# Prologue of an attention-and-experts layer: statistics, input sums and weight sums of the Strassen projection moved between engines, and the first group written anew

## The reference

```python
xn = layernorm(x)                                  # x: 2 x 2048 x 2048, over the last axis, fp32
q, k, v = split(xn @ Wqkv + bqkv)                  # 2048 -> 3 x 512
attn = softmax(q @ k.T / sqrt(512)) @ v
att = attn @ Wo + bo                               # 512 -> 2048
scores = (xn @ Wq.T) @ keys.T                      # 64 experts, router width 16
gate = softmax over the 16 largest of 64 scores, 0 elsewhere
z = (xn @ A.T).reshape(64, 8) * gate               # 64 experts of rank 8
out = x + att + 2 * z.reshape(512) @ B.T
```

## Time and profile before

| | |
|---|---|
| median of 3 runs | 2947.73 us (2945.4 to 2949.84) |
| time of the profiled execution | 2944.45 us |
| its span, first to last instruction | 2942.6 us |
| busy: PE / DVE / ACT / POOL | 94% / 63% / 32% / 25% of the span |
| chain of work that ended last | PE 74%, DVE 11%, DMA 5%, issue 4%, ACT 2%, POOL 2% |
| data moved | 476.34 MB, 162 GB/s on average; first fortieth of the span 373 GB/s |

### The profile page before, as it was taken

The page is one execution under the profiler, slowest core; times in us unless marked ns, Lnnn a source line. Parts: engine busy times, 40 slices in busy tenths (PEclk is TensorE's granted clock), DMA queues, the critical chain, the costliest instruction groups (busy, mean ns, idle before and its releaser), DMA issues.

```text
span 2942.6 us, 34127 instructions
## 1 busy us (share of the span) xinstructions
PE 2774.7 (94%) x12096; PEld 2252.9 (77%) x12096; DVE 1860.2 (63%) x2133; ACT 931.4 (32%) x1164; POOL 733.5 (25%) x429
## 2 busy tenths in 40 slices
PE   2888999999999999999979999999999999999999
PEld 1666787878778787888868787787887878878787
DVE  5776777676776777364565665656656565565653
ACT  1222232323232223322343343333433434334331
POOL 7165213020120303020030503305033050330511
PEclk8989999999999999999989999999999999999999
DMA  9667455544554554324524534545344353444544
GB/s 373 233 232 241 153 190 166 187 137 152 191 180 143 165 172 143 115 96 148 180 77 129 192 110 149 165 128 185 109 151 167 128 178 116 144 170 129 175 138 137
DMA packets 261611, 476.34 MB, mean 162 GB/s; under 512 B 26864, under 2 KB 76016, under 8 KB 257264
## 3 DMA queue, kind: packets, MB, share of 16 engines
q1 hardware_dynamic: 223408, 372.45, 38.8%
q10 hardware_dynamic: 29376, 68.72, 6.7%
q0 software_dynamic: 8704, 33.56, 3.2%
HBM read 390.74 MB, written 83.91 MB: 161 GB/s over the span
## 4 chain that ended last, share of the span: by engine, by line
PE 74%; DVE 11%; DMA 5%; issue 4%; ACT 2%; POOL 2%; SPq 2%; DVEq 0%; ACTq 0%; POOLq 0%
PE psum L694 30%; PE psum L1478 14%; PE psum L1480 13%; PE psum L1479 13%; DVE prob L1675 2%; DVE w_lo L744 2%; PE psum L631 2%; DVE r_lo L1647 2%; ACT r_hi L1359 1%; DMA t_scratch<-xb 1%; DVE s_lo L749 1%; SPq L363 1%; DVE part L731 1%; DMA w_raw<-t_scratch 1%; DVE xb L765 1%
## 5 line engine op out<-in xcount | busy, mean ns | idle before, releaser
L744 DVE TENSOR_TENSOR w_lo<-w_raw,w_hi 128x1024 fp32r<-128x1024 f32 x224 | 321.4, 1435 | 408.3 <-ACT w_hi L445 408.0
L445 ACT ACTIVATE w_hi<-w_raw 128x1024 fp32r<-128x1024 f32 x224 | 237.4, 1060 | 937.6 <-PE psum L694 807.1
L1647 DVE TENSOR_TENSOR r_lo<-r_raw,r_hi 128x1024 fp32r<-128x1024 f32 x256 | 383.1, 1510 | 190.4 <-ACT r_hi L1359 190.4
L1478 PE MATMUL psum<-r_hi,f_hi 128*128 128x512 f32 x1024 | 406.8, 397 | 27.6 <-DVE r_lo L1647 26.2
L1480 PE MATMUL psum<-r_hi,f_lo 128*128 128x512 f32 x1024 | 402.1, 393 | 0.0
L1479 PE MATMUL psum<-r_lo,f_hi 128*128 128x512 f32 x1024 | 402.1, 393 | 0.0
L694 PE MATMUL psum<-s_hi,w_hi 128*128 128x512 f32 x896 | 355.7, 397 | 43.4 <-DVE w_lo L744 30.2
L1613 POOL TENSOR_TENSOR res<-res,b_out 128x512 f32<-128x512 f32 x128 | 218.5, 1736 | 664.6 <-DMA res<-x 664.4
L694 PE MATMUL psum<-w_hi,s_hi 128*128 128x512 f32 x896 | 353.9, 395 | 27.8 <-DVE w_lo L744 27.8
L694 PE MATMUL psum<-w_lo,s_hi 128*128 128x512 f32 x896 | 352.3, 393 | 0.0
L694 PE MATMUL psum<-w_hi,s_lo 128*128 128x512 f32 x896 | 352.1, 393 | 0.0
(11 more groups left out here) (133 smaller groups left out, 4290.9 us busy)
## 6 DMA issues: line engine op xcount, KB each, us to landing
w_raw<-t_scratch SPq DMA_DIRECT2D x128, 512.0 KB, 3.9
w_raw<-W_blocks SPq DMA_DIRECT2D x96, 512.0 KB, 3.9
r_raw<-k_scratch SPq DMA_DIRECT2D x64, 512.0 KB, 3.8
r_raw<-v_scratch SPq DMA_DIRECT2D x64, 512.0 KB, 5.5
r_raw<-B_T SPq DMA_DIRECT2D x64, 512.0 KB, 3.9
res<-x SPq DMA_DIRECT2D x128, 256.0 KB, 4.9
r_raw<-Wo SPq DMA_DIRECT2D x64, 512.0 KB, 4.4
out<-res SPq DMA_DIRECT2D x128, 256.0 KB, 3.4
```

Source lines behind the costliest of these rows:

```text
L445: nc.scalar.activation(w_hi[:, s % RAW], w_raw[:, s % RAW], ACT.Copy).then_inc(s_whi, 1)
L744: nc.vector.tensor_tensor(w_lo[:, s % RAW], w_raw[:, s % RAW], w_hi[:, s % RAW].bitcast(F32), ALU.subtract).then_inc(s_wlo, 1)
L1478: pe.matmul(bank, sh, mh, start=first, stop=False)
L1647: nc.vector.tensor_tensor(r_lo[:, slot, :], r_raw[:, slot, :], r_hi[:, slot, :].bitcast(F32), ALU.subtract).then_inc(b_lo, 1)
```

## The change

- **Constants and first loads.** The host lays `WqT` out as 128 rows of 256 numbers, in the order in which the partitions hold them; SP issues the constants first, then weight 0 and weight 1 after the second and the fourth tile of `x` have landed. ACT loads block 0 of x behind the four tiles, and splits the router's weight before the first square root. DVE finishes the router's weight after its first tile.
- **Statistics.** For the tiles of groups 1 to 3, and for tiles 4, 6 and 7 of the first group, the sums are made by ACT (`moments`: Identity with a sum, mean, negated mean, Square with a sum, variance) instead of DVE; ACT no longer waits for DVE before a rows load. `STATS_AT` is spaced otherwise, and in the first group store and broadcast stand two items later.
- **Input sums.** s3, s4, s2 and s1 are made by DVE, in every group: in pass 1 (s3, s4), pass 4 (s2), pass 5 (s1); in the first group, pass 1, in the order of `MIX0`.
- **Weight sums.** In the first group DVE makes them from the `w_raw` that is there for the product anyway and one or two quarters that POOL has loaded: t3 beside pass 2, t4 and t2 beside pass 3, t1 beside pass 5. SP stores them. SP's reload of a `w_raw` slot waits for the sum as well.
- **GpSimd** issues transfers only: blocks 2 and 3 of x, then the 32 loads of weight quarters.

```diff
+SUMMED = {2: ("t3",), 3: ("t2", "t4"), 5: ("t1",)}
-STATS_AT = [(1, 1), (1, 2), (1, 3), (1, 4), (2, 1), (2, 2), (2, 3), (3, 1)]
+STATS_AT = [(1, 1), (1, 2), (1, 5), (2, 1), (2, 2), (2, 3), (2, 5), (2, 6)]
+MIX0 = [((2, 0),), ((3, 0), "s3"), ("s4", (2, 1)), ((3, 1), "s3"), ("s4", (2, 2)), ((3, 2), "s3"), ("s4", (2, 3)),
+        ((3, 3), "s3"), ("s4",)]
+OWN_AT = {(0, 3): 4, (0, 5): 6, (0, 6): 7}
...
         def load_w(g, idx, s):
             n = item(g, idx, s)
             wait(sp, s_wlo, n - RAW + 1)
+            if static(g) and g == 0:
+                i, k = (idx, s - RAW) if s >= RAW else (idx - 1, s - RAW + IPI)
+                if i in SUMMED:
+                    sp.wait_ge(s_tsum, t_number(i, k))
...
         def constants():
-            sp.dma_start(wq_raw[:], WqT.rearrange("(k p) r -> p k r", p=P)).then_inc(s_const, 16)
+            sp.dma_start(wq_raw[:].rearrange("p k r -> p (k r)"), WqT).then_inc(s_const, 16)
...
+        constants()
+        sp.wait_ge(s_row0[1], 16)
         load_w(0, 0, 0)
-        for p in range(PART):
-            sp.dma_start(x_pair(0, p), xT[2 * p * P:(2 * p + 2) * P, 0:W].rearrange("(a p) t -> p a t", p=P)
-                         ).then_inc(s_x[0][p], 16)
+        sp.wait_ge(s_row0[HT - 1], 16)
         load_w(0, 0, 1)
-        constants()
...
+        def moments(g, j):
...
+            chain = Chain(act, s_moments, base)
+            act.wait_ge(s_rows[j % 2], 16 * loads)
+            chain.link(nc.scalar.activation(tile, tile, ACT.Identity, accum_out=total[:, col]))
+            chain.step(nc.scalar.activation(mv[:, 0, col], total[:, col], ACT.Copy, scale=1.0 / C))
+            chain.link(nc.scalar.activation(less_mean[:, col], total[:, col], ACT.Copy, scale=-1.0 / C))
+            chain.link(nc.scalar.activation(tile, tile, ACT.Square, bias=less_mean[:, col], accum_out=squares[:, col]))
+            chain.link(nc.scalar.activation(var[:, col], squares[:, col], ACT.Copy, scale=1.0 / C))
+            act.sem_inc(s_amv, 1)
...
+        def sum_weights(idx, s):
+            dve.wait_ge(s_tload[s % PART], 16 * (t_uses(idx, s) + 1))
+            if idx == 3:
+                dve.wait_ge(s_tload1[s % PART], 16 * (s // PART + 2))
+                nc.vector.tensor_tensor(row_tile(s), w_raw[:, s % RAW], row_tile(s), ALU.add).then_inc(s_tsum, 1)
+                dve.wait_ge(s_tsum, t_number(3, s) - 1)
+                nc.vector.tensor_tensor(t_tile(3, s), t_tile(3, s), row_tile(s), ALU.subtract).then_inc(s_tsum, 1)
+            elif idx == 2:
+                nc.vector.tensor_tensor(t_tile(2, s), w_raw[:, s % RAW], t_tile(2, s), ALU.subtract).then_inc(s_tsum, 1)
...
+                        if s == 6:
+                            dve.wait_ge(s_mv, HT + 1)
+                            rstd_ready(len(OWN_AT), slice(HT, NTOK))
+                        if s == 7:
+                            rstd_finish(2, (HT + 1) * TILE_STEPS + RSTD_STEPS, slice(HT, NTOK))
...
+                    if not first and idx == 1 and 1 <= s <= PART:
+                        s3(g, s - 1)
+                        s4(g, s - 1)
+                    if idx == 4 and 1 <= s <= PART:
+                        s2(g, s - 1)
+                    if idx == 5 and 1 <= s <= PART:
+                        s1(g, s - 1)
...
+        def load_b21_b11(s):
+            stored(2, PART + s) if s < PART else stored(3, s - PART)
+            load_summand(3, s, "b21")
+            if s == 0:
+                pool.wait_ge(s_amv, len(OWN_AT) + NTOK)
...
+            pool.dma_start(row_tile(s), w_block("b11", s // PART, s % PART)).then_inc(s_tload1[s % PART], 16)
...
-        "WqT": np.ascontiguousarray(np.transpose(L0_ffn_Wq_w)),
+        "WqT": np.ascontiguousarray(np.transpose(L0_ffn_Wq_w).reshape(C // P, P, -1).transpose(1, 0, 2)).reshape(P, -1),
```

More of the change, by code:

```diff
@@ L164, in phase_a @@
     GATE_STEPS = 4 * HT + 6
-    T_ITEMS = 2 * HK
+    STAT_STEPS = 5
     def sb(name, shape, dt=F32):
@@ L490, in x_load, with rows_load @@
                           .rearrange("(a p) t -> p a t", p=P)).then_inc(s_x[block][p], 16)
-        def rows_load(g, j, tiles):
-            wait(act, s_tiles, tiles)
+        def rows_load(g, j):
             act.dma_start(rows[:, j % 2, :], x[bass.ds(g * TG + j * P, P), :]).then_inc(s_rows[j % 2], 16)
+        def moments(g, j):
+            tile = rows[:, j % 2, :]
+            col = slice(j, j + 1)
+            if static(g) and g == 0:
+                base, loads = max(j - HT - 1, 0) * STAT_STEPS, (j - HT) // 2 + 1
+            else:
+                base, loads = (g * NTOK - NTOK + len(OWN_AT) + j) * STAT_STEPS, g * HT - HT // 2 + j // 2 + 1
+            chain = Chain(act, s_moments, base)
[6 more added lines that the diff above has]
+            act.sem_inc(s_amv, 1)
         def square_roots(event, cols):
@@ L515, in scalar @@
             act.dma_start(first_rows(j), x[j * P:(j + 1) * P, :]).then_inc(s_row0[j], 16)
+        for p in range(PART):
+            x_load(0, 0, p)
+        act.wait_ge(s_const, 64)
+        act.wait_ge(s_wq, 1)
+        nc.scalar.activation(wq[:, :, 0:RD], wq_raw[:], ACT.Copy).then_inc(s_wq, 1)
         square_roots(1, slice(0, HT))
@@ L521, in scalar @@
                 split_weights(0, 0, 0)
-        rows_load(0, HT, 1)
-        rows_load(0, HT + 1, 0)
-        for p in range(PART):
-            x_load(0, 1, p)
         split_x(0, 0, 0)
@@ L550, in body @@
                         split_x(g + 1, 0, s - PART - 1)
+                    if first and (idx, s) in OWN_AT:
+                        moments(0, OWN_AT[idx, s])
                     if idx == 0 and s == PART - 1:
@@ L908, in norm_count @@
                 return NORM0.index((block, p)) + 1
+            if static(g) and g == 1:
+                return 4 * PART + NORM1.index((block, p)) + 1
             return g * 4 * PART + NORM.index((block, p)) + 1
@@ L935, in body @@
                         split_weights(g + 1, 0, 0)
+                    if first and (idx, s) == (2, 0):
+                        s4(0, PART - 1)
+                    if first and s + 1 < IPI and idx in SUMMED:
+                        sum_weights(idx, s + 1)
+                    if first and s + 1 == IPI and idx + 1 in SUMMED:
+                        sum_weights(idx + 1, 0)
                     if s == 0:
@@ L1100, in stored @@
+        for s in range(IPI):
+            load_b12(s)
+        for s in range(IPI):
+            load_b21_b11(s)
+        for s in range(IPI):
+            load_b22(s)
     def stored(engine):
```

311 lines of the change are left out of this document (156 added, 155 removed).

## The result

The changed kernel takes **2878.21 us**, median of 4 runs (2874.43 to 2878.93), against 2946.57 us before (4 runs, 2944.66 to 2949.84): a ratio of 0.9764, 95% interval 0.9747 to 0.9781. The forecast was 2868 us, with a range of 2840 to 2903. Its profiled execution took 2878.93 us, span 2877.1.

A forecast was written before the change was run, and what follows sets the result against it. PE was busy 94% of the span, so time could come only from stretches with PE idle or slow. The terms -9.5 - 25 - 10 - 10 - 5 - 17 = -76.5 us, against 2944.45, gave 2868 us; range 2840 to 2903.

The forecast's parts named there:

- The start: Up to the first product: earlier tiles and faster DVE additions bring it from 41.5 to 32 us, -9.5 us.
- pass 0: First group's pass 0: the 20.4 us wait for the router's weight goes; 78.0 to 53 us, -25 us.
- Pass 1: First group: 12.2 us new idle time behind store and broadcast, yet 72.8 to 63 us, -10 us.
- "1 us" for DVE's work behind the wait: Pass 1, after the broadcast: DVE's 4.8 to 7.2 us per item beside PE's 5.4 to 6.3 cost about 1 us.
- the rival with DVE as the bound: Passes 1 and 3: 16 items each take 1.5 us more, late loads +6; 2898 us; chance 0.14.
- Pass 3: First group: a late load costs 4 us, DVE's sums and gating 1.5; 57.2 to 52 us, -5 us.
- one late load: Pass 3's first sum needs a load POOL issues only after ACT's last moments; 4 us charged.
- Groups 1 to 3: Later groups: no DVE addition held up by POOL, 8 of 22.4 us of waits left, no slow spells; -17 us.
- ACT's cover: Groups 1 to 3: ACT's added 38 us of moments stay hidden behind 3.1 us of slack.
- The constants: Rival at the start: constants wait for bandwidth, not their rows; first product at 86 instead of 32; 2922 us; chance 0.06.
- POOL's issues: Costed at nothing; rival in pass 3: DVE holds them up, 3.3 us each; 2878 us; chance 0.03.
- the slower rival: Moments too long, in 27 places between weight copies; decides from about 10.3 us; at 11 us 2963 us; chance 0.02.

The follow-up runs named there:

- rows_behind: Changed kernel; first group's two 1 MB rows loads for the next group issued behind pass 1's statistics broadcast instead of between store and broadcast: 2870.56 us (0.9743).
- no_store_wait: Changed kernel; first group's second half of tokens normalised with the first half's statistics, broadcast three items later: 2871.14 us (0.9734).
- half_loads: Changed kernel; in pass 3 of the first group GpSimd loads only the first 128 of each 256 rows of b21 and b11: 2866.96 us (0.9726).
- half_sums: Changed kernel; in pass 3 of the first group an item's two sums cover 512 instead of 1024 columns: 2874.68 us (0.9752).
- sums_on_pool: Changed kernel; input sums s3, s4, s2, s1 of groups 1 to 3 back on GpSimd in the old order: 2913.14 us (0.9882).

## Why the prediction was right, and where it was not

**The start (-9.5, measured -10.6) and pass 0 (-25, measured -26.4).** Confirmed with their steps: the last statistics end at 20 us, the first additions take 1.22 us, ACT had the constants at 9.55 us. The wait for the router's weight went, and nothing as large came next.

**Pass 1 (-10, measured -3.7).** The new idle time was foreseen at its place: 13.3 us against 12.2. By the profile the store took 8.8 us instead of 11.5 and the broadcast 9.7 instead of 5.0: two errors that nearly cancel. The term fell short behind that: PE was idle 18.1 us instead of 14, since it also waited 4.1 us at the end of the pass for the router's result, and busy 51.0 instead of 49. The step that failed is "1 us" for DVE's work behind the wait. What came of it is mainly that wait of 4.1 us: DVE reads the router's result behind its normalising and its sums, and the first product of pass 2 waits for this. From the broadcast to the end of the pass DVE has hardly a gap, 44.16 of 47.22 us:

```profile
104.38:151.60 47.22, 39.51 (x160) 31.24 (x161) 44.16 (x39) 21.56 (x28) 2.17 (x3) 0.90 0.62 204
```

So here the rival with DVE as the bound had the mechanism, though not the 12 us that it charged for the pass. With DVE as the bound behind the wait, a us less of the wait is worth at least a us of the pass: rows_behind took 4.0 off the wait and 5.6 off the pass, no_store_wait 6.7 and 7.8.

**Pass 2 (-10, measured -9.5).** Confirmed.

**Pass 3 (-5, measured +11.8). This is the step that failed.** It counted DVE's instructions and one late load, "landing, at most the 6.8 us that twice the bytes take", and never the transfers of the pass as a whole. That could have been done from the rows: 0.5 MB of weight, 1 MB of quarters and 1 MB of sums an item are 20 MB (21.0 million bytes), and at the 378 GB/s of the start 55 us, longer than the 52 forecast, before results and chains are added. At the 330 GB/s that the pass reached it is 64 us, and all that moved in its 69.0 us is 22.8 million bytes. half_loads shows that the transfers are the bound; half_sums excludes DVE. The late load for which 4 us were charged cost DVE 1.97. The second part is the broadcast: it had 5 us in the sum for pass 1 and nothing for pass 3, where its store now takes 22.6 us instead of 11.1, in front of ACT's weights.

**Groups 1 to 3 (-17, measured -30).** The mechanism was right, the size too small. Of the 22.4 us of waits for low weights 4.0 are left, not 8, and waits of 3.5 us for a part (L924) went besides: 21.9 us. PE's busy time for the same matmuls, the slow spells after the waits, fell from 976.5 to 970.1 us in the three groups, 6.4 us, where the -17 left 2.6 for it beside 14.4 of waits. Together these are 28 of the 30 us. ACT's cover held: 133.55 of 325.4 us busy.

**The rest.** The 2 us more of passes 4 to 6 hold a wait of 1.53 us for a low weight just ahead of group 1.

**The rivals.** DVE as the bound was right for pass 1 in kind, and refuted for pass 3, which did become longer, but by its transfers. The constants came early. POOL's issues took 0.72 us in pass 3, with DVE making two additions an item: not held up, as the sum had it. The Trainium skill ("SBUF — State Buffer", section SBUF: two separate sides) states that GpSimd can't write its transfers' descriptors while DVE runs an instruction in a 2-port performance mode, and that an instruction with two inputs in SBUF competes only with a GpSimd instruction that reads SBUF. These additions have two inputs in SBUF, so for them it states no hold-up of the issues, and the trace agrees (0.72 us); that additions on both engines do hold each other up agrees as well (DVE's 2.62 us beside POOL in sums_on_pool). A tile of moments took 4.9 us, of which 1.91 and 2.01 are the two long instructions, far below the 10.3 us of the slower rival. The misses in passes 1 and 3, 23 us together, and the 13 us that the later groups gave beyond the forecast partly cancel: the total is nearer to the forecast than its terms are, and in so far its closeness, 10 us off, is luck.

## What to carry to other kernels

When work goes to an engine because its operands are there anyway, add up the bytes of the pass beside the instructions; here the instructions of pass 3 fitted beside the matmuls and its bytes did not. A small store on the path (statistics, a scale) took some 8 us even with few other transfers about (8.3 in rows_behind), and 23 beside many: let nothing that the next product needs stand behind its landing on the same engine. And an engine that computes rarely can still hold up another with every instruction: look for the longest of the neighbour's instructions of one shape beside their median, not at busy shares.
